# Ternary feed-forward stage of a six-block decoder: inner norm in the weights and the residual sum, with turning and projection one step earlier on two banks

## The reference

```python
def absmean(W):                      # ternary weights
    gamma = mean(abs(W)) + 1e-6
    Ws = W / gamma
    return sign(Ws) * minimum(round(abs(Ws)), 1.0)

h = einsum('btd,hd->bth', x, absmean(W_fc))       # 128 -> 512
h = gelu(h, approximate=False)
h = layernorm(h, ln_w, ln_b)                      # over the 512: the inner norm
y = einsum('bth,dh->btd', h, absmean(W_proj))     # 512 -> 128
x = _layernorm(x + y)                             # the outer norm, then the output
```

## Time and profile before

| what | value |
|---|---|
| runs | 386.26 us median of 3 (385.08 to 386.55) |
| profiled execution | 389.23 us, its span 387.4 us |
| mean granted TensorE clock | 0.949 |
| PE busy | 341.5 us, 88% |
| DVE busy | 250.6 us, 65% |
| ACT busy | 183.7 us, 47% |
| POOL busy | 186.1 us, 48% |
| chain that ended last | PE 67%, DVE 12%, issue 7%, POOL 6% |

### The profile page before, as it was taken

The page is one execution under the profiler, slowest core; times in us unless marked ns, Lnnn a source line. Parts: engine busy times, 40 slices in busy tenths (PEclk is TensorE's granted clock), DMA queues, the critical chain, the costliest instruction groups (busy, mean ns, idle before and its releaser), DMA issues.

```text
span 387.4 us, 9800 instructions
## 1 busy us (share of the span) xinstructions
PE 341.5 (88%) x3718; PEld 265.5 (69%) x3718; DVE 250.6 (65%) x592; ACT 183.7 (47%) x385; POOL 186.1 (48%) x267
## 2 busy tenths in 40 slices
PE   3789899998997089999996798999999999999982
PEld 2556566764897079999995665677777657766662
DVE  1799988888535413573335277845666668886894
ACT  2476567764468423233224243544435356667441
POOL 1867756554454515553313755311212465463673
PEclk9999999999579669999999699999999999999998
DMA  6799930000057111112111110000000000000000
GB/s 195 208 317 254 296 139 2 2 3 2 28 160 217 37 45 48 50 41 56 36 30 34 42 36 15 0 3 2 0 3 3 2 0 3 2 2 3 3 27 27
DMA packets 35938, 22.95 MB, mean 59 GB/s; under 512 B 4142, under 2 KB 33846, under 8 KB 35766
## 3 DMA queue, kind: packets, MB, share of 16 engines
q1 hardware_dynamic: 34582, 19.63, 17.6%
q0 software_dynamic: 1024, 2.10, 1.8%
q10 hardware_dynamic: 288, 0.62, 0.5%
HBM read 14.60 MB, written 7.73 MB: 58 GB/s over the span
## 4 chain that ended last, share of the span: by engine, by line
PE 67%; DVE 12%; issue 7%; POOL 6%; DMA 3%; ACT 2%; SPq 1%; POOLq 0%; DVEq 0%; ACTq 0%
PE banks L427 7%; PE banks L825 7%; PE banks L812 7%; PE banks L547 6%; PE banks L1505 6%; PE banks L1513 6%; PE banks L1536 5%; PE banks L524 4%; PE banks L856 3%; PE banks L1312 2%; PE banks L531 2%; POOL KB L671 2%; PE banks L508 2%; PE banks L371 2%; PE banks L496 2%
## 5 line engine op out<-in xcount | busy, mean ns | idle before, releaser
L671 POOL TENSOR_TENSOR KB<-KT,cst 128x512 f32<-128x512 f32 x48 | 49.3, 1047 | 7.4 <-DVE KT L631 5.6
L331 POOL TENSOR_SCALAR ve<-mv 128x1 f32<-128x1 f32 x40 | 10.6, 266 | 86.3 <-DVE mv L326 86.3
L436 ACT ACTIVATE PT<-banks 128x512 f32<-128x512 f32 x64 | 35.0, 595 | 24.5 <-PE banks L427 23.5
L401 DVE TENSOR_REDUCE mx<-banks 128x16 f32<-128x1024 f32 x32 | 38.6, 1207 | 5.4 <-PE banks L531 4.7
L1528 DVE TENSOR_TENSOR PT<-banks,PR 128x512 f32<-128x512 f32 x23 | 15.9, 691 | 40.4 <-PE banks L1513 35.8
L862 ACT ACTIVATE U<-banks 128x512 f32<-128x512 f32 x40 | 23.9, 597 | 38.0 <-PE banks L825 22.6
L1493 POOL COPY U<-WALL 128x1024 f32 x21 | 21.8, 1040 | 37.7 <-PE banks L1513 36.2
L427 PE MATMUL banks<-cst,PR 128*128 128x128 f32 x256 | 36.6, 288 | 0.5 <-POOL PR L891 0.5
L417 ACT ACTIVATE PR<-PR 128x1024 f32<-128x1024 f32 x32 | 33.8, 1057 | 3.4 <-DVE PR L411 3.2
L812 PE MATMUL banks<-XT,WQKV 128*128 128x128 f32 x256 | 33.3, 293 | 0.4 <-ACT XT L1713 0.4
L812 PEld LDWEIGHTS banks<-XT,WQKV 128*128 128x128 f32 x256 | 31.8, 206 | 1.1 <-ACT XT L1713 0.7
(11 more groups left out here) (183 smaller groups left out, 700.2 us busy)
## 6 DMA issues: line engine op xcount, KB each, us to landing
routed_rows<-zero SPq DMA_DIRECT2D x1, 4544.0 KB, 20.4
U<-in_L_ffn_wg_dram SPq DMA_DIRECT2D x8, 256.0 KB, 4.5
U<-in_L_ffn_wu_dram SPq DMA_DIRECT2D x8, 256.0 KB, 4.9
U<-in_L_ffn_wd_dram SPq DMA_DIRECT2D x8, 256.0 KB, 5.4
U<-in_L_attn_W_qkv_dram SPq DMA_DIRECT2D x1, 1536.0 KB, 23.0
XG<-routed_rows SPq DMA_DIRECT2D x23, 64.0 KB, 1.8
routed_rows<-YS SPq DMA_DIRECT2D x23, 64.0 KB, 1.6
cst<-shape_constants ACTq DMA_DIRECT2D x1, 537.0 KB, 4.4
```

What stands on the lines that cost most here:

```text
L401: dve.tensor_reduce(mx[:, n % 2, :], s, AX.X, ALU.max).then_inc(self.max.sem, 1)
L436: act.activation(PT[:, n % 2, 4 * m:4 * m + 4, :].rearrange("p r q -> p (r q)"), PS[:, B_PT + m, :], ACT.Copy).then_inc(self.pt.sem, 1)
L671: pool.tensor_tensor(KB[:, n % 2, b], bc(KT[:, n % 2, b, :], 1, 8), bc(cst[:, C_HEAD:C_HEAD + 8], 2, SEQ), ALU.mult).then_inc(self.kb.sem, 1)
```

## The change

The inner norm is (h - mean) * rstd * w + b. The mean over the 512 hidden values is subtracted from the weights instead: every row of the scaled projection weights gets its column mean taken off, since projecting h - mean is the same as projecting h with weights whose sum over the 512 is zero. Four matmuls with a matrix of -1/512 make those means in bank B_PT (`means_pe`), VectorE adds them to FCT (`center`). The factor rstd is one number per token, so it multiplies the projected row in the residual sum (`scalar_tensor_tensor` in `r_dve`). L1022 and its buffer FN go. The transposes read the output of gelu.

The steps of a ternary tile become: transposes and copy in 19+i (`t_pe`, `pt_act`), projection in 20+i (`vb_pe`) alternately into banks B_K and B_Q, residual sum in 20+i, outer norm in 21+i. In a step of VectorE the norm of a ternary tile now comes after the residual sum of the next one. `summed` and `turned` give lists, since in step 20 a tile of the attention stage and one of the ternary stage are summed. The small statistics buffer gets four slots. ScalarE copies the turned tile before it makes the next gelu. The core of the diff:

```diff
+                dve.wait_ge(s_tern, 2)
+                dve.tensor_scalar(MEAN, cst[:, C_ONES:C_ONES + P], -1.0 / INNER, None, ALU.mult).then_inc(self.blocks.sem, 1)
...
+            def means_pe(self, pe):
+                pe.wait_ge(*self.scaled.at(CH))
+                pe.wait_ge(*self.blocks.at(2))
+                for c in wide.vo_cp:
+                    pe.wait_ge(*c.at(2))
+                for c in range(CH):
+                    m = pe.matmul(PS[:, B_PT, 0:P], MEAN, FCT[:, 1, c, :], start=(c == 0), stop=(c == CH - 1))
+                m.then_inc(self.means.sem, 1)
+
+            def center(self, dve):
+                dve.wait_ge(*self.means.at(1))
+                dve.tensor_tensor(FCT[:, 1], FCT[:, 1], bc(PS[:, B_PT, 0:P], 1, CH), ALU.add).then_inc(self.centered.sem, 1)
+
+            def r_dve(self, dve, job):
+                i = job.i
+                dve.wait_ge(*self.o_mm.at(i + 1))
+                dve.wait_ge(*self.res.at(i + 1))
+                dve.wait_ge(*self.rstd.at(i + 1))
+                dve.scalar_tensor_tensor(R[:, i % 2, :], PS[:, (B_K, B_Q)[i % 2], 0:P], hst[:, i % 4, 13:14], XR[:, i, :],
+                                         ALU.mult, ALU.add).then_inc(self.norm.r.sem, 1)
+                dve.wait_ge(*self.norm.r.at(i + 1))
+                self.norm.stats(dve, i, R[:, i % 2, :])
...
             def exp_act(self, act, job):
                 i = job.i
                 act.wait_ge(*self.h_mm.at(i + 1))
                 if i >= 2:
-                    act.wait_ge(*self.n.at(i - 1))
+                    act.wait_ge(*self.st.at(i - 1))
+                    act.wait_ge(*self.t_mm.at(i - 1))
                 act.activation(FH[:, i % 2, :], PS[:, B_S + i % 2, :], ACT.Gelu).then_inc(self.gelu.sem, 1)
...
-            def hidden_dve(self, dve, job):
+            def t_pe(self, pe, job):
                 i = job.i
-                dve.wait_ge(*self.rstd.at(i + 1))
-                if i >= 2:
-                    dve.wait_ge(*self.t_mm.at(i - 1))
-                dve.tensor_scalar(FN[:, i % 2, :], FH[:, i % 2, :], hst[:, i % 2, 8:9], hst[:, i % 2, 13:14],
-                                  ALU.subtract, ALU.mult).then_inc(self.n.sem, 1)
-                dve.wait_ge(*self.n.at(i + 1))
-
-            def va_pe(self, pe, job):
-                i = job.i
-                pe.wait_ge(*self.n.at(i + 1))
+                pe.wait_ge(*self.gelu.at(i + 1))
...
-            def o_pe(self, pe, job):
+            def vb_pe(self, pe, job):
                 i = job.i
                 pe.wait_ge(*self.ht.at(i + 1))
...
+                if i >= 2:
+                    pe.wait_ge(*self.norm.r.at(i - 1))
+                else:
+                    for s in job.ago(i + 1).stage.qk_read(NT - 1):
+                        pe.wait_ge(*s)
                 for c in range(CH):
-                    m = pe.matmul(PS[:, B_OX, P:2 * P], FT[:, i % 2, c, :], FCT[:, 1, c, :], start=(c == 0), stop=(c == CH - 1))
+                    m = pe.matmul(PS[:, (B_K, B_Q)[i % 2], 0:P], FT[:, i % 2, c, :], FCT[:, 1, c, :], start=(c == 0), stop=(c == CH - 1))
                 m.then_inc(self.o_mm.sem, 1)
...
             t, w = at(tiles, j - 5), at(tiles, j - 4)
-            return w if w and w.stage.wide else t if t and not t.stage.wide else None
+            return [k for k, early in ((t, False), (w, True)) if k and k.stage.early == early]
...
-                r = summed(tiles, j)
-                if r:
+                for r in summed(tiles, j):
                     r.stage.r_dve(dve, r)
-                if hidden:
-                    t.stage.hidden_dve(dve, t)
+                for x in ternary:
+                    x.stage.ln_dve(dve, x)
...
                 fc.project_bias(pe)
+                fc.means_pe(pe)
                 pe.wait_ge(*fc.bias.at(1))
                 self.turn_pe(pe, (0,))
...
                 for t in range(2):
                     self.combine(dve, t)
                     self.apply(dve, t)
+                fc.center(dve)
...
         def post_pe(pe, j, late):
+            if j == 2 and not late:
+                pe.wait_ge(*fc.centered.at(1))
```

More of the change, by code:

```diff
@@ L353, in decoder_kernel @@
             blocks_pool = cos_pool = hidden_pool = bias_pool = shares_pool = none
-            wide = False
+            wide = early = False
             def qkw_copies(self, eng, part, job):
@@ L366, in x_pe @@
                     pe.wait_ge(*self.norm.r.at(i + 2))
-                elif job.after is not None and not self.wide:
+                elif job.after is not None and not self.wide and not job.after.stage.early:
                     pe.wait_ge(*job.after.stage.norm.r.at(1))
@@ L703, in decoder_kernel @@
         class Wide(Stage):
-            wide = True
+            wide = early = True
             def __init__(self, name):
@@ L1033, in va_pe, with pt_act @@
                 for c in range(CH):
-                    m = pe.transpose(PS[:, B_PT + i % 2, P * c:P * (c + 1)], FN[:, i % 2, P * c:P * (c + 1)], ident)
+                    m = pe.transpose(PS[:, B_PT + i % 2, P * c:P * (c + 1)], FH[:, i % 2, P * c:P * (c + 1)], ident)
                 m.then_inc(self.t_mm.sem, 1)
-            def ya_act(self, act, job):
+            def pt_act(self, act, job):
                 i = job.i
@@ L1059, in x_act @@
                 pass
+            early = True
         class Tile:
@@ L1174, in stream_pe @@
                     b.stage.qk_pe(pe, b)
-                x = turned(tiles, j)
-                if x:
+                for x in turned(tiles, j):
                     x.stage.x_pe(pe, x)
@@ L1217, in stream_dve @@
                     y.stage.y_dve(dve, y)
-                t, x = at(tiles, j - 3), turned(tiles, j)
+                t = at(tiles, j - 3)
                 hidden = t and isinstance(t.stage, Ternary)
@@ L1221, in stream_dve @@
                     t.stage.sum_dve(dve, t)
-                if x:
+                ternary, others = [], []
+                for x in turned(tiles, j):
+                    (ternary if isinstance(x.stage, Ternary) else others).append(x)
+                for x in others:
                     x.stage.ln_dve(dve, x)
```

23 lines of the change are left out of this document (8 added, 15 removed).

## The result

The changed kernel takes 379.63 us (median of 22 runs, 378.33 to 384.65) against 385.89 us before (22 runs). The ratio is 0.983 [0.982, 0.984], a gain of 6.6 us. The profiled execution took 379.86 us, its span is 377.9 us, with a mean granted clock of 0.966 against 0.949.

A forecast was written before the change was run, and what follows sets the result against it. VectorE was taken to bound the ternary steps at 2.49 us. Steady steps and one step less give -4.0, the wide stage's front 0: profiled 389.23 becomes 385.2, timed runs 3 us lower, 382.3; range 379.7 to 384.8.

The forecast's parts named there:

- 0.56 us of inner norm: VectorE's steady ternary step: without the inner norm 2.49 us becomes 1.99, so TensorE sets the pace at 2.28.
- the new sum: Residual sum with a scalar on VectorE: 0.35 us against 0.29 for the plain sum.
- the new work in front of the wide stage: Matmuls of the means (1.16 us) and weight correction (0.7 us), both covered by idle time: cost 0.
- The end: After the last hidden projections: tile 7's starts at 373.09, the last norm at 380.54 instead of 384.53.
- The clock in front of the wide stage: TensorE's clock falls again in the gap before the wide stage, L812 still at 6.4 us.
- The first rival: Clock stays up in front of the wide stage, L812 at 3.8 us: 379.7 to 380.3 us, chance 0.11.
- The second rival: Ternary steps keep 2.5 us, as sum, statistics and gelu follow TensorE's step end: 384.8 us, chance 0.12.
- slower third one: A two-step loop over the added waits takes 5.7 us instead of 4.1: 387 to 389 us, chance 0.04.
- steps 20 and 21: Overlap with the attention tiles: step 20 ends 0.4 us later, step 21 loses a 0.05 pause, net +0.35.
- the pure step: TensorE's steady ternary step, same work as before: 2.28 us.

The follow-up runs named there:

- e3: Changed kernel with the inner norm folded, but turning, projection and sum in the steps of before, four gelu buffers: 391.9 us, ratio 0.997 to the kernel before.
- f1: Changed kernel once more, no edit, on another chip: 379.95 us, ratio 0.983 to the kernel before.
- f2: Kernel before once more, no edit, beside the changed kernel on another chip: 386.19 us, ratio 1.001.
- e1: Kernel before plus four unused two-pass matmuls, shaped like the means, in TensorE's gap in front of the wide stage: 393.25 us, ratio 0.999.
- i2: Kernel before once more, no edit, where it needs 386 us: 385.7 us, ratio 0.995.
- i1: Kernel before plus four unused transposes of tile 0's gelu in step 19's pause, where the kernel before needs 386 us: 384.72 us, ratio 0.995.
- h3: Changed kernel once more, no edit, where the kernel before needs 392 us: 387.16 us, ratio 0.989.
- g1: Kernel before plus four unused transposes of tile 0's gelu in step 19's pause, where the kernel before needs 392 us: 392.53 us, ratio 1.000.
- e4: Changed kernel plus three unused 512-column matmuls around the means, in the gap in front of the wide stage: 389.15 us, ratio 0.990 to the kernel before.
- e2: Changed kernel without the matmuls of the means and the correction of the weights: 387.57 us, ratio 0.987 to the kernel before.

## Why the prediction was off in size

**Where it was right.** VectorE was the bound in the step of the earlier trace rows and its 0.56 us of inner norm a lever, but it paid only together with the earlier step (e3). TensorE took over as the pace, VectorE waited for the projection, the new sum cost 0.35, and the new work in front of the wide stage was covered (f1 and f2 are equal at L812). The end was priced well: from the start of tile 7's hidden projection to the last norm 7.45 us were forecast and 7.52 measured (367.56 to 375.08). The reading of the earlier trace rows was wrong there, though: at 377.7 VectorE was not full but waited for GpSimd's root. The forecast holds that gain, 1.16 us between the last two sums, without naming it.

The clock in front of the wide stage fell again, as forecast. The first rival's 379.7 to 380.3 is near the time, but by luck: its mark, L812 at 3.8 us, did not appear in the change (6.0 us), and e1 gave nothing. The second rival (2.5 us a step) and the slower third one did not occur.

**First step that failed: steps 20 and 21, forecast +0.35, measured -0.2.** The chain of before, beside the earlier trace rows:

```profile
360.76 0.86 PE banks L983 x2
...
366.10 0.92 PE banks L983 x2
```

Step 20 takes 363.50 - 360.76 = 2.74 us before and 358.85 - 356.02 = 2.83 after, 0.09 longer where I had 0.4. Step 21 takes 366.10 - 363.50 = 2.60 before and 361.15 - 358.85 = 2.30 after, 0.30 shorter where I had 0.05. I had put L371 at 0.30 in both kernels; behind a projection without a pause it is 0.11, in each of the two steps.

**Second: the pure step, forecast 2.28, measured 2.19.** I took it that the same work on TensorE takes the same time. In the old order it does: e3, with the fold and the old steps, needs 0.86 + 0.99 + 0.44 = 2.29 us, as the earlier trace rows have 2.28. In the new order it is 0.44 + 0.89 + 0.86 = 2.19. The projection takes 0.99 us in front of the transposes and 0.89 in front of the hidden projection; why is not shown. From tile 4's hidden projection to tile 7's this makes 6.57 us instead of 6.81.

These account for the stage: 0.55 us in steps 20 and 21 and 0.24 in the three after them, less 0.07 at the end, where the last norm starts 1.97 us after the last sum instead of 1.89. That is 0.72, the distance from -4.0 to -4.7.

**Third, and put at nothing: TensorE's clock outside the gap of the wide stage.** The profile that I worked from had no fall in the ternary stage, and I took the clock of one execution for that of the median one. In f2 and i2 a fall there makes the stage 35.3 and 35.2 us instead of 34.1. How many of the timed executions have it is not known. Where the kernel before needs 386 us the runs suggest 1.1 us [0.3, 1.5] for it (i1), but 0.7 [-0.3, 1.4] against i2 alone.

**The sum.** The time came out 2.7 us under the forecast. 0.7 is the stage. 0.4 is the start: the kernel before has a median of 385.89 in 22 runs and not the 386.26 of three. About 1.6 us are left, of which the clock may be 1.1; the rest stays open. Where the kernel before needs 392 us there is nothing left over: the gain is 5.0 us, or 4.4 by the ratio (h3), against 4.7 from the stage.

Open too is why the front is up to 8 us longer in some executions than in f2. The traces say where: up to the matmul that f2 starts at 90 us all profiles agree within a microsecond, and they part between there and the expert stage. There the clock is low for 17.0 us in the first profile after and in f1 and f2, and for 30.8 in the first profile before and in i2, whose expert stage starts 3.2 us later than f2's. That is not all of it, since g1 has 23.9 us of low clock and starts that stage 6.9 us later than f2.

## What to carry to other kernels

Taking an operation off the engine that is the bound moved the stage by 0.9 us; the other 3.8 came when the pipeline's depth shrank by one step. Price both separately. When an engine becomes the pace in a new order of its work, its step of before need not be its step of after (2.28 and 2.19 us here). Cut two traces at the same instructions before comparing their spans: here 4.8 of 9.5 us lay in front of the stage that changed and were scatter. And when a pause of TensorE is filled, look at more than one profile of the kernel before: a fall of the clock that only some executions have can be in the median without being in the trace at hand.

## What the runs showed of the hardware

The clock fell although TensorE was far from idle: in f2 it had been busy for 1.36 of 1.90 us and fell two microseconds later, at 355.9, while it was working. The fall did not follow the pauses at once: in f2 and in i2 TensorE had by then been busy again for 1.6 and 2.2 us. The same two pauses, at 357.77 to 358.97 in the first profile of the kernel before, had no fall behind them: the chain gives L547 1.04 us and L983 0.86 us right after. The place in the run doesn't decide it either: in that profile and in i2 the stage starts at the same 353.3 us, and one has the fall and the other not.

In the gap of the wide stage 1.16 us of matmuls saved nothing (e1), and filling it moved the fall behind the next pause (e4). The Trainium skill (TensorE: Matmul & The Clock Gate, Why this matters for your kernels) advises against long idle gaps between bursts of matmuls; the fall that comes with the undivided gap of 4.5 us in the kernel before and in e2 agrees. But e1 has the same fall of 6.8 us with idle stretches of only 1.90 and 1.54 us, so dividing a gap was not enough.
